# Ahead of layer 0 of a graph transformer: the plan's squares on VectorE, fewer histogram steps beside the counts, histogram and first tiles mixed 9 to 8

## The reference

```python
xn = layernorm(x, ln1_g[l], ln1_b[l])
deg = segment_sum(ones, src, n)               # how often a node is a source (and its own loop)
deg = (deg - deg.mean()) / (std(deg, ddof=1) + 1e-6)
pos = xn @ Wpos[l] + bpos[l] + deg[:, None] * Wdeg[l][0] + bdeg[l]
xp  = xn + pos
q, k, v = (xp @ W + b  for W, b in ((Wq, bq), (Wk, bk), (Wv, bv)))
att = clip(sum(q[dst] * k[src]) / scale, -50, 50)     # 8 heads of 16
alpha = softmax of att over the edges of a target
x = x + segment_sum(v[src] * alpha, dst) @ Wo[l] + bo[l]
x = x + gelu(layernorm(x, ln2_g[l], ln2_b[l]) @ W1[l] + b1[l]) @ W2[l] + b2[l]
out = layernorm(x0 + x)                                # after both layers, x0 the input
```

## Time and profile before

| engine | busy us | share of the span | instructions |
|---|---|---|---|
| TensorE, matmul | 2966.6 | 78% | 23989 |
| TensorE, weight load | 2291.0 | 60% | 23989 |
| VectorE | 2846.9 | 75% | 6650 |
| ScalarE | 1703.6 | 45% | 4253 |
| GpSimd | 2572.7 | 67% | 2665 |

### The profile page before, as it was taken

How to read it: one execution, slowest core, us unless ns; L and a number is a source line. 1 busy time by engine, 2 the same in 40 slices (tenths; PEclk the granted TensorE clock), 3 DMA queues, 4 the chain that set the end, 5 groups by cost and what they waited for, 6 DMA issues and landing times.

```text
span 3811.8 us, 71274 instructions
## 1 busy us (share of the span) xinstructions
PE 2966.6 (78%) x23989; PEld 2291.0 (60%) x23989; DVE 2846.9 (75%) x6650; ACT 1703.6 (45%) x4253; POOL 2572.7 (67%) x2665
## 2 busy tenths in 40 slices
PE   4874688888888888888776567778788787887876
PEld 3653566666666666666554356666566566666664
DVE  9886678788888788888774466777777777767774
ACT  1331235454545454545444135455454454544544
POOL 4007777777777777777752777777777777777770
PEclk6785689998989898999986678998898998889885
DMA  3015445555555455555542445555555555555540
GB/s 103 2 52 157 117 144 171 149 168 150 169 153 165 146 169 157 169 161 169 156 123 69 118 140 157 162 164 163 155 166 153 164 161 158 164 156 164 164 145 25
DMA packets 392799, 542.97 MB, mean 142 GB/s; under 512 B 77981, under 2 KB 304858, under 8 KB 392238
## 3 DMA queue, kind: packets, MB, share of 16 engines
q0 software_dynamic: 126720, 346.20, 31.1%
q1 hardware_dynamic: 258208, 184.95, 16.1%
q10 hardware_dynamic: 7506, 7.20, 0.6%
HBM read 512.93 MB, written 25.14 MB: 141 GB/s over the span
## 4 chain that ended last, share of the span: by engine, by line
POOL 44%; PE 19%; issue 17%; DVE 14%; ACT 3%; DMA 2%; SPq 0%; DVEq 0%; POOLq 0%; ACTq 0%
POOL kv_ring L1901 33%; POOL arena L1901 11%; PE psum L889 3%; PE psum L767 2%; DVE scratch L1595 2%; DVE att L1604 2%; DVE work L1307 2%; PE psum L1000 2%; PE psum L930 2%; PE psum L979 1%; PE psum L946 1%; PE psum L792 1%; DVE scratch L1619 1%; DVE arena L1645 1%; PE psum L1054 1%
## 5 line engine op out<-in xcount | busy, mean ns | idle before, releaser
L1901 POOL DMA_INDIRECT kv_ring<-kv_table,src_idx x1984 | 1897.9, 957 | 727.8 <-issue 599.7
L1160 ACT ACTIVATE scratch<-psum 128x512 f32<-128x512 f32 x1108 | 623.2, 570 | 540.7 <-PE psum L899 349.6
L1901 POOL DMA_INDIRECT arena<-kv_table,src_idx x656 | 624.0, 951 | 203.2 <-issue 196.5
L1595 DVE TENSOR_TENSOR scratch<-psum,kv_ring 128x512 f32<-128x512 f32 x496 | 318.7, 684 | 433.1 <-DMA kv_ring<-kv_table,src_idx 407.4
L930 PE MATMUL psum<-q_win,scratch 64*128 64x128 f32 x5280 | 446.3, 316 | 211.6 <-DVE scratch L1595 178.1
L930 PEld LDWEIGHTS psum<-q_win,scratch 64*128 64x128 f32 x5280 | 378.5, 216 | 330.4 <-issue 280.9
L1604 DVE TENSOR_REDUCE att<-scratch 128x64 f32<-128x1024 f32 (+1 forms) x442 | 519.5, 1175 | 0.1
L889 PE MATMUL psum<-arena 128*128 128x256 f32 x1568 | 458.7, 419 | 55.6 <-ACT arena L1171 53.8
L946 PE MATMUL psum<-scratch 128*64 128x136 f32 x5280 | 440.9, 317 | 23.6 <-DVE work L1791 8.3
L1193 ACT ACTIVATE psum<-att 128x64 f32<-128x64 f32 (+1 forms) x442 | 100.3, 227 | 682.5 <-DVE att L1610 675.5
L1171 ACT COPY arena<-psum 128x512 f32<-128x512 f32 x448 | 231.1, 532 | 385.4 <-PE psum L889 379.2
(11 more groups left out here) (253 smaller groups left out, 4637.8 us busy)
## 6 DMA issues: line engine op xcount, KB each, us to landing
arena<-kv_table SPq DMA_DIRECT2D x112, 896.0 KB
kv_ring<-kv_table,src_idx POOLq DMA_INDIRECT x1984
q_win<-q_table SPq DMA_DIRECT2D x660, 32.0 KB
work<-kv_table SPq DMA_DIRECT2D x98, 128.0 KB
arena<-kv_table,src_idx POOLq DMA_INDIRECT x656
q_win<-q_table SPq DMA_DIRECT2D x112, 64.0 KB
work<-q_table SPq DMA_DIRECT2D x98, 64.0 KB
kv_table<-work SPq DMA_DIRECT2D x49, 128.0 KB, 2.4
```

What stands on the lines that cost most here:

```text
L1160: e.activation(to[:, at:at + width], apart[k % 2][:, 0:width], ACT.Relu, bias=1.0, scale=-1.0).then_inc(apart_read, 1)
L1595: e.tensor_tensor(prod[:, ts[0] * P:(ts[-1] + 1) * P].rearrange("p (t d) -> p t d", d=D), q_edge[f % 2][:, 0:len(ts) * P].rearrange("p (t ...
L1901: e.indirect_dma_start(kv[m % RING_KV][:, t, :], None, kv_table[l], bass.IndirectOffsetOnAxis(ap=src_idx[:, c * T + t:c * T + t + 1], axis ...
```

## The change

1. The five instructions of the squares move from GpSimd (`plan_edges`) to VectorE (`plan_squares`), behind the third histogram step of the phase. The wait on `seg_turned` goes, since VectorE has passed it already.
2. HEAD_START goes from 8 to 3: the count loop has 9 passes and three histogram steps (0 to 2), the phase behind the statistics has 46.
3. ScalarE's five plan writes move from ahead of the first tiles to behind tile 8's turn (PLAN_BY).
4. On TensorE there are 8 tiles to 9 products (EARLY_BY = 8, 9): tiles 0 to 40 among the products, 41 to 49 behind them. The first total stands behind tile 41, the second behind tile 44 (DEGREE_BY = 3).
5. VectorE's degree chain waits no longer for all tiles' normalization, and the row updates wait for the copies of their own group (`early_copy` at `hi`) instead of all 49.

```diff
--- before.py
+++ after.py
@@ -58,11 +58,14 @@
 RUN = 8
 RUNS = 10
 HSTEPS = NC * T // HG
-HEAD_START = 8
+HEAD_START = 3
 
 RUN_HI = 4
 
-EARLY_BY = 5, 4
+EARLY_BY = 8, 9
+
+PLAN_BY = 8
+DEGREE_BY = 3
 OUT_TILES = 6
 NEWTON = 3
 RSQRT_MAGIC = float(0x5F3759DF)
@@ -806,9 +809,8 @@
                     m = e.transpose(psum[:, (0, 1, 3, 4)[g], i * NS:(i + 1) * NS],
                                     seg_src[:, (4 * g + i) * P:(4 * g + i + 1) * P], ident[0:NS, 0:NS])
                 m.then_inc(seg_turned, 1)
-            for s in range(max(COUNT_STEPS, HEAD_START + COUNT_FIRST)):
-                if s < COUNT_STEPS:
-                    count_product(e, s)
+            for s in range(COUNT_STEPS):
+                count_product(e, s)
                 if COUNT_FIRST <= s < HEAD_START + COUNT_FIRST:
                     hist_product(e, s - COUNT_FIRST)
             e.wait_ge(weights_ready, 2)
@@ -838,12 +840,15 @@
                 while tile * EARLY_BY[1] < (s - HEAD_START + 1) * EARLY_BY[0] and tile < NT + 1:
                     early_tensor(e, tile)
                     tile += 1
+
+            asked = 0
             for i in range(tile, NT + 1):
                 early_tensor(e, i)
-            e.wait_ge(deg_ask, 1)
-            e.matmul(total, ones[:], one[:, 0:1], start=True, stop=True).then_inc(deg_got, 1)
-            e.wait_ge(deg_ask, 2)
-            e.matmul(total, ones[:], one[:, 2:3], start=True, stop=True).then_inc(deg_got, 1)
+                if asked < 2 and (i == tile + asked * DEGREE_BY or i == NT):
+                    asked += 1
+                    e.wait_ge(deg_ask, asked)
+                    e.matmul(total, ones[:], one[:, 2 * asked - 2:2 * asked - 1], start=True, stop=True).then_inc(deg_got, 1)
+            assert asked == 2
 
         def plan_of(e, n, first):
 
@@ -1110,6 +1115,12 @@
                     e.wait_ge(plan_out, 16 * PLAN_ROWS)
                 e.copy(first_qkv(j, j + 1)[:, 0, :], psum[:, 3 + j % 2, 0:QKV]).then_inc(early_copy, 1)
 
+        def write_plan(e):
+            e.wait_ge(edge_ready, 5)
+            to = plan_table.rearrange("(q i) (k h) n -> k q i h n", i=2, h=2)
+            for k, part_of in enumerate((plan_low, plan_own, plan_sum, plan_query, plan_qsum)):
+                e.dma_start(to[k], part_of.rearrange("q (i h n) -> q i h n", i=2, h=2)).then_inc(plan_out, 16)
+
         def scalar_first(e):
             e.dma_start(seg_dst, dst.rearrange("(p k) -> p k", p=NS)).then_inc(seg_dst_in, 16)
             chunks = dst.rearrange("(a c n) -> a c n", a=1, n=CH)
@@ -1142,14 +1153,12 @@
             for l in range(L):
                 e.wait_ge(w_folded, l + 1)
                 e.copy(w_qkv[:, l, :], psum[:, l, 0:QKV]).then_inc(w_copied, 1)
-            e.wait_ge(edge_ready, 5)
-            to = plan_table.rearrange("(q i) (k h) n -> k q i h n", i=2, h=2)
-            for k, part_of in enumerate((plan_low, plan_own, plan_sum, plan_query, plan_qsum)):
-                e.dma_start(to[k], part_of.rearrange("q (i h n) -> q i h n", i=2, h=2)).then_inc(plan_out, 16)
             e.wait_ge(first_stats, 1)
             e.wait_ge(weights_ready, 2)
             for i in range(NT + 2):
                 early_scalar(e, i)
+                if i == PLAN_BY:
+                    write_plan(e)
             first_tables(e, 1)
 
         def one_hots(e, to, n, what, h):
@@ -1350,9 +1359,8 @@
             e.tensor_copy(n_src_b, n_sh).then_inc(count_step, 1)
             e.tensor_scalar(n_dst_b, n_dh, -float(JB), None, ALU.add).then_inc(count_step, 1)
             e.wait_ge(count_step, 4)
-            for s in range(max(COUNT_STEPS, HEAD_START + COUNT_FIRST)):
-                if s < COUNT_STEPS:
-                    count_step_hot(e, s)
+            for s in range(COUNT_STEPS):
+                count_step_hot(e, s)
                 if s == COUNT_FIRST - 1:
                     source_digits(e)
                 if COUNT_FIRST <= s < HEAD_START + COUNT_FIRST:
@@ -1437,6 +1445,17 @@
             e.wait_ge(tiles_counted, 1)
             step(e.tensor_scalar, seg_dst, seg_dst, GROUP - 1, None, ALU.bitwise_and)
             e.tensor_scalar(edge_group, edge_group, HALF // GROUP - 1, None, ALU.bitwise_and).then_inc(edges_placed, 1)
+
+        def plan_squares(e):
+
+            e.wait_ge(part_cast, 2)
+            e.tensor_tensor(plan_qsum, plan_low, plan_low, ALU.mult).then_inc(edge_ready, 1)
+            e.tensor_tensor(plan_sum, plan_own, plan_own, ALU.mult).then_inc(edge_ready, 1)
+            e.tensor_tensor(group_square, plan_query, plan_query, ALU.mult).then_inc(edge_ready, 1)
+            e.wait_ge(edge_ready, 2)
+            e.tensor_tensor(plan_sum, plan_sum, plan_qsum, ALU.add).then_inc(edge_ready, 1)
+            e.wait_ge(edge_ready, 4)
+            e.tensor_tensor(plan_qsum, plan_qsum, group_square, ALU.add).then_inc(edge_ready, 1)
 
         def plan_starts(e, step):
 
@@ -1548,11 +1567,12 @@
                 if s == HEAD_START:
                     plan_starts(e, step)
                     plan_chunks(e, step)
+                if s == HEAD_START + 2:
+                    plan_squares(e)
                 if s == HEAD_START + 4:
                     plan_offsets(e, step)
             e.wait_ge(hist_sum, HSTEPS)
             e.wait_ge(pool_step, 9)
-            e.wait_ge(early_norm, NT)
             step(e.scalar_tensor_tensor, out=deg, in0=counts, scalar=1.0, in1=valid, op0=ALU.add, op1=ALU.mult)
             e.tensor_reduce(one[:, 0:1], deg, AX_X, ALU.add).then_inc(deg_ask, 1)
             e.wait_ge(deg_got, 1)
@@ -1566,8 +1586,8 @@
             step(e.tensor_scalar, one[:, 6:7], one[:, 4:5], one[:, 3:4], 1e-6, ALU.mult, ALU.add)
             step(e.reciprocal, one[:, 7:8], one[:, 6:7])
             step(e.tensor_scalar, deg_z[:], dev, one[:, 7:8], None, ALU.mult)
-            e.wait_ge(early_copy, NT)
             for i, to, columns, n, lo, hi in table_parts:
+                e.wait_ge(early_copy, hi)
                 for j in range(lo, hi):
                     row = first_qkv(j, j + 1)[:, 0, columns]
                     e.scalar_tensor_tensor(out=row, in0=wz[:, columns], scalar=deg_z[:, j:j + 1], in1=row,
@@ -1846,18 +1866,6 @@
                         sort_vector(e, s, k)
 
 
-        def plan_edges(e):
-
-            e.wait_ge(part_cast, 2)
-            e.wait_ge(seg_turned, 4)
-            e.tensor_tensor(plan_qsum, plan_low, plan_low, ALU.mult).then_inc(edge_ready, 1)
-            e.tensor_tensor(plan_sum, plan_own, plan_own, ALU.mult).then_inc(edge_ready, 1)
-            e.tensor_tensor(group_square, plan_query, plan_query, ALU.mult).then_inc(edge_ready, 1)
-            e.wait_ge(edge_ready, 3)
-            e.tensor_tensor(plan_sum, plan_sum, plan_qsum, ALU.add).then_inc(edge_ready, 1)
-            e.wait_ge(edge_ready, 4)
-            e.tensor_tensor(plan_qsum, plan_qsum, group_square, ALU.add).then_inc(edge_ready, 1)
-
         def pool_first(e):
             e.iota(iota_i, pattern=[[1, P]], base=0, channel_multiplier=0).then_inc(pool_step, 1)
             e.memset(ones[:], 1.0).then_inc(pool_step, 1)
@@ -1882,7 +1890,6 @@
                             channel_multiplier=-1).then_inc(sort_tables, 1)
             e.affine_select(out=one_tile[:], in_=ones_b[:, 0:2 * ST], pattern=[[1, 2 * ST]], compare_op=ALU.is_equal, fill=0.0,
                             base=-(ST - 1), channel_multiplier=0).then_inc(sort_tables, 1)
-            plan_edges(e)
             e.wait_ge(deg_ask, 1)
             e.memset(plan, 0.0).then_inc(plan_ones, 1)
             e.wait_ge(plan_ones, 1)
```

## The result

The changed kernel takes 3828.23 us (median of 20 runs, 3821.37 to 3850.81) against 3819.14 before (20 runs, 3813.87 to 3828.11). The ratio is 1.0028, with a 95% interval of 1.0019 to 1.0038: slower by 9 to 11 us where 21 less were forecast. The profiled execution took 3830.03 us, its span is 3828.3.

A forecast was written before the change was run, and what follows sets the result against it. The work ahead of layer 0's first gather was taken to set that gather's start, the rest following unchanged. The terms, -13.7 - 17.7 + 5.6 + 4.6 = -21.2 us, gave 3799 us, 8-in-10 range 3787 to 3812.

The forecast's parts named there:

- Term A: Count loop ahead of the weights: five histogram steps leave it, a gain of 13.7 us (bounds 10 to 15.7).
- term B: VectorE from weights to bn_stats: with the squares off GpSimd its nine instructions run free, a gain of 17.7 us.
- lock-step reading: Weight instructions: VectorE is held in step with GpSimd's products, 3.44 us for a two-input instruction on 128x2 elements.
- rival 2: Weight instructions on VectorE: slow of themselves, so the squares only change their engine; time 3816, chance 5%.
- Term C: Histogram phase: 46 steps at VectorE's pace, squares 5.9 and clock 5 included, 166.3 us, a loss of 5.6.
- rival 1: Loop of 46 products: TensorE's clock stays low throughout, 0.87 us a step; time 3836, chance 7%.
- a clock at 0.50 beyond 150: Histogram phase: TensorE's clock still at 0.50 beyond 150 us would show the forecast wrong.
- Term D: Degree chain up to the rows: tiles ahead of the totals make it 7.1 us instead of 2.55, a loss of 4.6.
- The front: All that lies ahead of the first gather: the gather was to start 21 us earlier, at 271 us.
- behind it stand the gathers and the edge work of both layers, which the diff leaves alone: Behind the first gather: nothing changes, so an earlier row update is an earlier gather.
- Rival 3: Behind the first gather: part of the 21 us is given back; half 3809, two thirds 3813; chance 12%.

The follow-up runs named there:

- r1_after: The changed kernel, unchanged, on a chip where every version takes 5590 to 5750 us; ratio to before 0.9970.
- r2_after_mem5: The changed kernel with five memsets of one element on GpSimd where the squares stood; 3825.8 us in one run, against 3812.6 for before.
- r3_after_ttf1: The changed kernel with one small f32 tensor_tensor on GpSimd behind its affine_selects; timed on another chip at 3808.5 us, ratio to before 0.9979.
- r4_after_ttf_early: The changed kernel with one small f32 tensor_tensor on GpSimd ahead of the three affine_selects; 3806.3 us in one run, against 3817.7 for before.
- r3_after_tt5_mix54: The changed kernel with five small tensor_tensor on GpSimd, 5 tiles to 4 products and both totals behind all tiles; ratio to before 0.9988.
- r3_after_tt5_mix11: The changed kernel with five small tensor_tensor on GpSimd and one tile to one product; ratio to before 0.9972.

## Why the prediction was wrong

**Term A (13.7) and term B (17.7): right.** 14.0 (59.62 to 45.63) and 17.5 (20.2 to 2.7 us). The lock-step reading of the earlier trace rows was the cause. With the squares' move alone, and HEAD_START still 8 (r1_before_vecsq), the nine instructions take the same 2.7 us:

```profile
65.36 0.28 DVE L1307 TENSOR_SCALAR arena<-arena 128x256 f32<-128x256 f32 x1
...
68.08 9.57 DVE L1535 BATCH_NORM_STATS2 scratch<-x_all 128x6 f32<-128x128 f32 x49
```

With the squares put back on GpSimd (r1_after_poolsq) `bn_stats` begins at 64.04 instead of 48.51 (r1_after). There it was mostly the count's one-hots that were held: four of them take 14.16 us. The Trainium skill, "SBUF — State Buffer", "Who interferes with whom", has this right. That the `tensor_scalar` ones were held too does not go beyond it, as the prediction has it: the same section of the Trainium skill lists `tensor_scalar` among the instructions that can contend with GpSimd. The Trainium skill, "Perfetto Trace Analysis", "Optimizing Scalar/DVE Operations", offers GpSimd for a saturated VectorE and warns that it might not help; here the warning held, as rival 2 did not happen.

**Term C (a loss of 5.6): 9.1.** 69.56 to 239.41 is 169.9 us, 166.3 was the sum. The squares were 5.8 as taken. VectorE's waits for TensorE in the phase (us in total, times, longest):

```profile
DVE kv_ring L1333 <- PE psum L770: 5.7, 7, 0.9
```

5 had been put down for the clock, so the size came out, by luck. What failed is that the clock, once up, stays up (under rival 1: "it did rise with the same instructions, and stayed"), which I had read from a phase in which TensorE was the bound and carried over to one in which it is not. The late rise cost 2.2 and not 5, as the clock was up at 115.8; the fall from 150 to 170 cost the other 3.5, and a clock at 0.50 beyond 150 was one of my signs of being wrong. Most of what is left, some 2.6 us, is VectorE's own pace: 3.19 us a step over 46 steps and not 3.13 (an estimate: 169.9 less the waits, the plan, the offsets, the squares and the last product).

**Term D (a loss of 4.6): 9.2.** The count of tiles ahead of each total was right: in the three profiles whose clock was at 1.00 from 240 to 250 (r2_after_mem5, r3_after_ttf1, r4_after_ttf_early) the rows began 10.1 us after the last sum, 10.8 being the forecast. In the changed kernel they began 15.3 after it, as the tail ran at the lower level. I had that in the bounds (7) and not deep enough.

**The front: 13.2 in the profiled pair, not 21.2.** And the pair flatters it. The kernel before has its first gather at 292.0 and 288.5 in two profiles, and at 285.8 with five small instructions more on GpSimd (r2_before_tt5); the clock rose at 146.9, 132.7 and 123.4 in the three. Some of the spread is the clock's. The changed front with the squares on VectorE and 8 to 9 lies at 281.2 in the mean of its twelve profiles. So the front gives some 7.5 us, a third of what I forecast, and the one profile that I had was the latest of these three.

**The step that gave the wrong sign** is the sentence "behind it stand the gathers and the edge work of both layers, which the diff leaves alone". The diff leaves their instructions alone, but not their duration. Rival 3 (given back behind the first gather) had the right place and neither cause nor size: it allowed for two thirds of the front, and 29.7 us were given back of 13.2. Of 20 profiles the five with no computing instruction on GpSimd but `fold` and its iotas, memsets and affine_selects have medians of 953 or 957, the fifteen others 946 or 949. With 2640 gathers 7 to 11 ns are 18 to 29 us. Less 7.5 of the front that gives a loss of 11 to 21, an estimate; 9 and 17 were measured (20 and 6 runs).

**Open.** Why a small computing instruction on GpSimd makes 2640 later gathers 7 ns shorter is not shown. It does so in bf16 and f32, as a `tensor_tensor` or a `tensor_copy`, alone or five times, ahead of or behind the three affine_selects, and the large squares do it too; five memsets do not. It is not shown either why `fold` does not: it is a `tensor_tensor` of 128x64 that stands in all five programs with the longer gathers. It runs at 1.7 us, ahead of the memsets, and the others at 3.4 us or later; no run puts a small one beside `fold`. Something that lasts from the first gather to the last remains, and the profile has no row for it. Of the clock it is shown that it falls behind a pause of TensorE, and not why the low stretches that end ahead of the last sum last from 3 to 51 us, with TensorE busy again.

## What to carry to other kernels

Where one engine issues thousands of like instructions and sets the pace, compare the shortest and the median duration of that one group before and after any change, however far away the change is: 11 ns of 946 were twice the gain at the front in the profiled pair. A sum over a front says nothing of the rest of the kernel until that group's row has been held against it. And a clock read in a phase bound by TensorE does not carry over to the same instructions when another engine sets the pace; read it in a phase of the new kind, or put both levels into the sum. Where a clock falls, look at the few microseconds ahead of the fall: the busy share of the stretch behind it does not show the pause.

## What the runs showed of the hardware that I had not expected

- An indirect gather's duration has levels: medians of 946, 949, 953 and 957 ns in twenty profiles, each constant through its execution. It can be one level apart between two executions of one kernel (changed: 957, 953, 953; with one small f32 `tensor_tensor`: 946, 949), and on one chip between two kernels with the same program on GpSimd (r3_after_tt5_mix54 946, r3_after_tt5_mix11 949).
- TensorE's granted clock fell from 1.00 to 0.50 behind single pauses of 0.20 to 1.27 us, 40 times in the twenty profiles, and stayed low for up to 51 us with the engine busy again (r3_after_tt5_mix11, 121 to 172). With 5 tiles to 4 products it never fell while tiles were left.
- Where GpSimd and VectorE held each other up, it was at times the one and at times the other: before, GpSimd's first square took 28.20 us and VectorE's one-hots kept their pace; in r1_after_poolsq that square took 10.68 and four one-hots 14.16.
- On two chips the kernel before took 5650 and 5710 us instead of 3820. On the one where it was profiled its gathers took the same 946 ns and the first began at 288.5.
